# A recurrent layer with routed experts on one core: second relus of left-over expert jobs on ScalarE, a later lay-out of the extra slots, and four output buffers

## The chip, the cores and the metric

One core of a Trainium2 chip runs the whole program. The metric is the device time of one execution in microseconds, and the numbers compared are medians over several executions. All arithmetic is in 32-bit floats but for a few small tables in bf16. Engines are named as the profile names them: PE is TensorE (PEld its weight loads), DVE is VectorE, ACT is ScalarE, POOL is GpSimd, SP is SyncE; ACTq, SPq are the DMA queues that ACT and SP issue to.

## What is computed

The input is 8 sequences of 512 tokens with 128 features. Each layer half is preceded by a layer norm with a scale and a shift that depend on the sequence, and its output is multiplied by a gate and added to the input.

```python
for each of 512 time steps:                      # 8 sequences at once
    h_ssm = silu(h_ssm @ A.T + bx)               # 64 states
    r, z  = sigmoid(...), sigmoid(...)
    n     = tanh(i_n + r * h_n)
    h_rnn = (1 - z) * n + z * h_rnn              # 128 states
    out   = g0 * (h_ssm @ Cw.T + Cb + dx) + g1 * (h_rnn @ proj_w.T + proj_b)
x = x + ga * out
h = layernorm(x) * (1 + cb) + sb
expert_idx = argmax(softmax(h @ gate_w.T))       # one of 8 experts for each of 4096 tokens
y = relu(h @ w1[e] + b1[e]) @ w2[e] + b2[e]      # 128 -> 512 -> 128
x = x + gb * y * prob[e]
```

## The kernel before

**Steps and tiles.** The time steps are a chain, so the program is written as a loop over steps u (`steps`, U_END = 622 of them). Steps 0 to 511 each do one recurrent step; 16 of them make a tile of 128 tokens (16 steps by 8 sequences), tile c being steps 16c to 16c+15. Norms, routing and expert work of earlier tiles are placed by tables of step numbers into the steps of later tiles. From step 512 on there is no recurrence, only the rest of the expert work; I call these steps the tail. Every engine runs its own instruction list in the order in which the loop emits it, and the engines are held together by semaphores alone: a step number is a place in the lists, not a time.

**Experts.** Tiles 0 to 30 are dispatched in five groups (SIZE = 6, 7, 7, 6, 5). Each token's row is scattered by POOL into a block of its expert in a DRAM table (`rows`). A slot is one 128-row block of one expert. Slots 0 to 53 serve groups 0 to 3; in the last group slots 54 to 61 are fixed, one for each expert, and 62 to 65 are the extra slots, whose experts are found at run time. Tile 31 isn't scattered: each expert is applied to it whole and the results are gated and summed in `acc`.

**A slot's units.** On PE a slot is nine matmul units: X transposes the rows, A and C are the first layer in two halves, D and B the second layer; each of A, B, C, D has a first (hid_bank_a, hid_a) and a second part (hid_bank_b, hid_b). The table UNITS (`schedule`) says which units stand in which step. After X, ACT copies the bank to xT. After each A and C part a relu leaves PSUM: the first part always on ACT (L787), the second on DVE (L1176) unless the unit is in the set ON_ACT, which sends it to ACT (L783). After B, DVE adds the bias and evicts to y_sb (L1190), and SP stores it to `rows` (`store_y`, L623). Units are planned in `schedule` one by one while the recurrence runs; what is left of a group at step 512 (here the left-over jobs: slots 49 to 53 of group 3) is listed from step 512 on, three units a step, and the last group from step 526, mostly two a step.

**Lay-out.** Ten small DVE instructions per group (`lay_out`, L1055 to L1088: over, n_slots, end_slot, passed, expert_f, ended, first_f, block_f, place, expert) find the experts and blocks of the slots. `dispatch_at` gives their steps. `rows_at` is the step after them, from which SP loads (`load_expert`, L589 on): it reads the expert number, copies that expert's weights from w_all to wx (578 KB, L599), reads the block number and loads the rows (L604 or L607). SP's list is in order, so a store of y_sb listed behind such a load leaves after it. The rows of the fixed slots (`load_fixed`, L615) stand at step 513.

**Results.** A finished group is gathered by POOL, tile by tile, into yg (`gather`, four buffers; it first waits until all of the group's y_sb stores have landed). DVE makes fin_g (L1196) and o_sb (L1201) in steps FINAL_AT and OUT_AT; the tile is stored three steps later, in the tail by ACT (`store_out`, L854). o_sb has two buffers, so the o_sb of tile j waits for the store of tile j-2.

```python
def dispatch_at(k, n):
    at = (last_tile(k) + 2) * T
    return at + (2 + n if at < NT * T else 1 + n // 3)
```

Of the kernel before, what the change touches and what calls it, by code (L numbers as in the profile page):

```python
# [88 lines left out]
NBUF = 7  # L89
ND = 4  # L90
RING = 12
W_EXP = 2 * FC * P + FC + P

ENDED = (2, 2, 0, 0, 0, 0, 0, 0, 0, 1, 1, 0, 0, 0, 1, 0)
# [56 lines left out]
def dispatch_at(k, n):  # L151

    at = (last_tile(k) + 2) * T
    return at + (2 + n if at < NT * T else 1 + n // 3)


def scatter_at(j):
# [3 lines left out]
def rows_at(k):  # L161
    return dispatch_at(k, DISPATCH_STEPS - 1) + 1
# [19 lines left out]
def schedule():  # L182

    at, on_act, ready, act_ops, dve_used, relu_open = {}, set(), {}, {}, {}, set()

    def may(event, u, place):
        return event in ready and ready[event] <= (u, place)  # L190

    def ok(unit, u, place, first):
        kind, n, h = unit
        new = n == first
        if kind == "X":
            return new or may(("C", n - 1, 0), u, place)
        if kind == "A":
            return may(("X", n, 0), u, place) and (new or (may(("C", n - 1, h), u, place) and ("D", n - 1, h) in ready))
        if kind == "C":
            return may(("A", n, h), u, place) and ("A", n, 1) in ready and (new or ("B", n - 1, h) in ready)  # L200
        if kind == "D":
            return may(("A", n, h), u, place) and (new or may(("B", n - 1, 1), u, place))
        return may(("C", n, h), u, place) and ("D", n, 1) in ready

    def dve_room(u):
        return 270 if u // T < DVE_EARLY.get(u % T, 0) else DVE_ROOM[u % T]

    def home(unit, u, place):


        kind, n, h = unit
        if kind == "D" or unit[0::2] == ("B", 0):
            return "PE"
        if (kind == "B" or kind != "X" and h) and dve_used.get(u, 0) + DVE_COST[kind == "B"] <= dve_room(u):
            return "DVE"
        if kind != "B" and act_ops.get(u + (place > 0), 0) < ACT_ROOM[(u + (place > 0)) % T]:
            return "ACT"
        return None

    u = 0  # L220
    for k in range(NG - 1):
        first, end = SLOT0[k], SLOT0[k + 1]
        head = {"X": [], "A": [], "B": [], "C": [], "D": []}
        for unit in order_of_units(k):
            head[unit[0]].append(unit)
        u = max(rows_at(k) + 4, u)
        while any(head.values()) and u < NT * T:
            place = 0
            while place < ROOM - taken(u):
                for kind in PICK[place > 0]:  # L230
                    unit = head[kind][0] if head[kind] else None
                    where = home(unit, u, place) if unit and ok(unit, u, place, first) else None
                    if where:
                        break
                else:
                    break
                head[kind].pop(0)
                at.setdefault(u, []).append(unit)
                ready[unit] = (u, place + 1)
                if where == "ACT":  # L240
                    act_ops[u + (place > 0)] = act_ops.get(u + (place > 0), 0) + 1
                    ready[unit] = (u + (place > 0) + 1, 0)
                    if unit[2]:
                        on_act.add(unit)
                if where == "DVE":
                    dve_used[u] = dve_used.get(u, 0) + DVE_COST[kind == "B"]
                    ready[unit] = (u + 1, 1)
                if kind in "AC" and unit[2]:
                    relu_open.update(range(u, ready[unit][0] + ready[unit][1]))
                place += 1  # L250
            u += 1


    def room(u):
        return 3 if u < NT * T + T else 2

    u, used = NT * T, 0
    for k in range(NG):
        if rows_at(k) + 4 > u:
            u, used = rows_at(k) + 4, 0  # L260
        for i, what in enumerate(order_of_units(k)):
            if what in ready:
                continue
            if i == 1:
                u, used = u + 1, 0
            while used >= room(u):
                u, used = u + 1, 0
            at.setdefault(u, []).append(what)
            used += 1
    return at, on_act, relu_open  # L270


# [19 lines left out]
def final_steps():  # L292


    gather, final, u, f = {}, {}, 0, 0
    for k in range(NG):
        done = Y_STEP[SLOT0[k + 1] - 1]
        for i in range(SIZE[k]):
            u = max(u + 1, done + 4)
            if u < NT * T:  # L300
                u += min((14 - u) % T, (5 - u) % T if k >= 2 else T)
            if u >= NT * T:
                u = max(u, gather[FIRST[k] + i - 1] + (9 if k < NG - 1 else 3), NT * T + 13)
            gather[FIRST[k] + i] = u
            f = max(f + 1, u + (4 if u < NT * T else 12))
            final[FIRST[k] + i] = f
    return gather, final

# [9 lines left out]
def adaln_kernel(nc, x, silu_in, weights, ssm_weights, w1, b1, w2, b2, col_bias, bias_a, bias_b,  # L318
                 bias_const, const, out):
    ctx = ExitStack()  # L320
    with ctx:
        def sb(name, shape, dt=F32):
            return ctx.enter_context(nc.sbuf_tensor(name, shape, dt))
# [4 lines left out]
        def sem(name):  # L328
# [103 lines left out]
        y_sb = sb("y_sb", [P, NBUF, P])  # L432
        yg = sb("yg", [P, 4, P])
        fin_g = sb("fin_g", [P, P])
        o_sb = sb("o_sb", [P, 2, P])
        gate = sb("gate", [P, E])
        acc = sb("acc", [P, P])

# [55 lines left out]
        gate_ready, acc_step = sem("gate_ready"), sem("acc_step")  # L494
        w2_done, y_ready, fin_step, o_ready, stored = (
            sem("w2_done"), sem("y_ready"), sem("fin_step"), sem("o_ready"),
            [sem("stored0"), sem("stored1")])

        def ge(eng, s, n):

# [61 lines left out]
        def _(eng):  # L562
# [71 lines left out]
            def step(u, c, q, t):  # L634
# [11 lines left out]
                for j in range(NS):  # L646
                    if u == OUT_AT[j] + 3 and OUT_AT[j] < TAIL:
                        ge(eng, o_ready, j + 1)
                        eng.dma_start(out[:, j * P:(j + 1) * P], o_sb[:, j % 2, :]).then_inc(stored[j % 2], 16)

            steps(step)
            for q in range(2):
                eng.wait_ge(stored[q], 16 * NT // 2)


        @block.gpsimd
# [73 lines left out]
        def _(eng):  # L730
# [120 lines left out]
            def store_out(j):  # L851

                ge(eng, o_ready, j + 1)
                eng.dma_start(out[:, j * P:(j + 1) * P], o_sb[:, j % 2, :]).then_inc(stored[j % 2], 16)  # L854

            eng.wait_ge(seed_step, SEED_STEPS)
            eng.wait_ge(bank_filled, 3)
# [15 lines left out]
        def _(eng):  # L873
# [216 lines left out]
            def step(g, c, q, t):  # L1090
# [101 lines left out]
                for j in range(NS):  # L1192
# [4 lines left out]
                                                       in1=mod_gb, op0=ALU.mult, op1=ALU.mult).then_inc(fin_step, 1)  # L1197
                    if g == OUT_AT[j]:
                        ge(eng, fin_step, j + 1)
                        ge(eng, stored[j % 2], 16 * (j // 2))  # L1200
                        nc.vector.tensor_tensor(o_sb[:, j % 2, :], fin_g[:, :], x_sb[:, j * P:(j + 1) * P],  # L1201
                                                ALU.add).then_inc(o_ready, 1)

            steps(step)
# [2 lines left out]
            ge(eng, o_ready, j)  # L1207
            nc.vector.tensor_tensor(fin_g[:, :], acc[:, :], mod_gb, ALU.mult).then_inc(fin_step, 1)
            ge(eng, fin_step, j + 1)
            ge(eng, stored[j % 2], 16 * (j // 2))  # L1210
            nc.vector.tensor_tensor(o_sb[:, j % 2, :], fin_g[:, :], x_sb[:, j * P:(j + 1) * P],
                                    ALU.add).then_inc(o_ready, 1)


# [290 lines left out]
```

## Time and profile before

| | |
|---|---|
| median of 3 runs | 701.41 us (700.33 to 702.38) |
| profiled execution, its own time | 703.28 us |
| its span | 701.3 us |
| busy PE / PEld / DVE / ACT / POOL | 98% / 92% / 76% / 61% / 17% |
| PE's matmul instructions | 13868 |
| granted clock of PE, mean | 0.995 |
| chain that ended last, share of PE | 95% |

Times of rows are microseconds from the start of the span. "Busy" is time inside instructions; the part in brackets at a row's end is how long the engine had been idle before it, and what released it. PE rows merge neighbours of one kind, and a row x4 is one unit. The last recurrent step ends at 633.5; the tail is the rest.

### The profile page before, as it was taken

The numbers are of one execution on the slowest core, as the hardware profiler recorded it, in microseconds if no ns is written. First come the engines' busy times: TensorE is split into PE (matmuls) and PEld (weight loads), VectorE is DVE, ScalarE is ACT, GpSimd is POOL, SyncE is SP. The second block draws the span as 40 slices with busy tenths as digits, with TensorE's granted clock in tenths as the row PEclk, the third lists the DMA queues.
The fourth block names the chain that finished last, engine by engine and source line by source line (L and its number), as shares of the span: only waits on it lengthen the run. The fifth ranks groups of instructions, "written<-read, shape, count | busy, mean of one in ns | idle before, by whom it ended". The sixth has DMA issues, their size and how long they took to land.

```text
span 701.3 us, 35723 instructions
## 1 busy us (share of the span) xinstructions
PE 685.8 (98%) x13868; PEld 643.3 (92%) x13868; DVE 535.9 (76%) x3226; ACT 427.4 (61%) x2678; POOL 121.2 (17%) x209
## 2 busy tenths in 40 slices
PE   7999999999999999999999999999999999998896
PEld 5899999999999999999999999999999999997795
DVE  4777777777787777887888788878877878877455
ACT  4555555555766666567666665766667666664342
POOL 4011111111101111112121112121212122211202
PEclk9999999999999999999999999999999999999998
DMA  8915000604431100054221001633110353333411
GB/s 303 364 72 207 7 7 7 243 10 156 165 123 60 43 15 11 14 207 168 97 93 56 22 19 49 240 127 111 55 63 15 127 176 105 101 105 129 131 47 51
DMA packets 45659, 71.97 MB, mean 103 GB/s; under 512 B 6157, under 2 KB 28499, under 8 KB 45363
## 3 DMA queue, kind: packets, MB, share of 16 engines
q1 hardware_dynamic: 41490, 64.38, 26.1%
q0 software_dynamic: 1984, 4.07, 2.1%
q8 instruction: 110, 1.80, 1.1%
q10 hardware_dynamic: 2016, 1.25, 0.6%
q14 instruction: 59, 0.48, 0.2%
HBM read 14.31 MB, written 21.04 MB: 50 GB/s over the span
## 4 chain that ended last, share of the span: by engine, by line
PE 95%; DMA 1%; DVE 1%; SPq 1%; issue 1%; ACT 0%; POOLq 0%; DVEq 0%
PE rs_bank L1220 34%; PE nz_bank L1220 24%; PE hid_bank_b L1220 12%; PE work L1220 11%; PE y_bank L1220 8%; PE hid_bank_a L1220 7%; DMA out<-o_sb 1%; DMA yg<-rows,pos 0%; SPq L623 0%; DMA rows<-y_sb 0%; DVE fin_g L1196 0%; DVE hid_b L1176 0%; SPq L599 0%; SPq L598 0%; SPq L602 0%
## 5 line engine op out<-in xcount | busy, mean ns | idle before, releaser
L1220 PE MATMUL nz_bank<-h_ring,wg 128*64 128x16 f32 x4088 | 207.2, 211 | 0.0
L1220 PE MATMUL rs_bank<-s_ring,ws_sb 128*64 128x128 f32 x1024 | 195.1, 272 | 0.0
L795 ACT ACTIVATE r_fac<-rs_bank 128x8 f32<-128x8 f32 x512 | 91.6, 179 | 168.7 <-PE rs_bank L1220 161.6
L1220 PEld LDWEIGHTS nz_bank<-h_ring,wg 128*64 128x64 f32 x4088 | 160.7, 136 | 1.6
L1220 PE MATMUL rs_bank<-mw,wg 128*64 128x8 f32 x2044 | 146.7, 202 | 0.0
L1220 PE MATMUL rs_bank<-u,wg 128*64 128x8 f32 x2044 | 140.3, 206 | 0.0
L1220 PEld LDWEIGHTS rs_bank<-s_ring,ws_sb 128*64 128x64 f32 x1024 | 127.2, 136 | 9.1
L1101 DVE TENSOR_TENSOR_SCAN nz_bank<-r_fac,nz_bank 128x16 f32<-128x16 f32 x512 | 99.7, 195 | 46.2 <-ACT r_fac L795 30.4
L1105 DVE SCALAR_TENSOR_TENSOR mw<-v_fac,h_ring 128x8 f32<-128x8 f32 x512 | 85.6, 167 | 57.8
L1220 PEld LDWEIGHTS rs_bank<-mw,wg 128*64 128x64 f32 x2044 | 103.2, 135 | 18.9 <-DVE mw L1105 4.9
L801 ACT ACTIVATE v_fac<-nz_bank 128x8 f32<-128x8 f32 x512 | 91.1, 178 | 42.3
L1220 PEld LDWEIGHTS rs_bank<-u,wg 128*64 128x64 f32 x2044 | 101.8, 135 | 1.0
L1112 DVE SCALAR_TENSOR_TENSOR h_ring<-mw,u 128x8 f32<-128x8 f32 x512 | 85.4, 167 | 17.4
L803 ACT ACTIVATE n_fac<-nz_bank 128x8 f32<-128x8 f32 x512 | 91.0, 178 | 1.7
L1109 DVE SCALAR_TENSOR_TENSOR u<-v_fac,n_fac 128x8 f32<-128x8 f32 x512 | 85.6, 167 | 2.0
L798 ACT ACTIVATE s_ring<-rs_bank 64x8 f32<-64x8 f32 x512 | 80.9, 158 | 0.4 <-PE rs_bank L1220 0.4
L1220 PE MATMUL hid_bank_b<-w_sb,const_sb 128*64 128x128 f32 (+1 forms) x592 | 74.9, 322 | 0.0
L692 POOL DMA_INDIRECT rows<-h_ring,pos x31 | 31.7, 1022 | 243.9 <-DVE h_ring L1112 241.2
L676 POOL TENSOR_TENSOR ve<-mv,eps 128x1 f32<-128x1 f32 x64 | 16.9, 265 | 224.9 <-DVE mv L888 224.9
L787 ACT ACTIVATE hid_a<-hid_bank_a,wx 128x128 f32<-128x128 f32 x116 | 42.6, 367 | 11.0 <-PE hid_bank_a L1220 9.8
L1220 PE MATMUL hid_bank_b<-xT,wx 128*64 128x128 f32 x464 | 47.7, 280 | 1.0 <-DVE hid_b L1176 1.0
L1220 PE MATMUL hid_bank_a<-xT,wx 128*64 128x128 f32 x464 | 48.1, 281 | 0.2
(181 smaller groups left out, 1129.1 us busy)
## 6 DMA issues: line engine op xcount, KB each, us to landing
wx<-w_all SPq DMA_DIRECT2D x58, 578.0 KB, 3.5
rows<-zeros SPq DMA_DIRECT2D x3, 4096.0 KB, 14.5
rows<-y_sb SPq DMA_DIRECT2D x66, 64.0 KB, 1.8
w_all<-in_w SPq DMA_DIRECT2D x2, 2048.0 KB, 15.4
xs_sb<-rows SPq DMA_DIRECT2D x54, 64.0 KB, 3.0
x_sb<-in_x SPq DMA_DIRECT2D x1, 1920.0 KB, 8.8
out<-o_sb SPq DMA_DIRECT2D x19, 64.0 KB, 2.5
out<-o_sb ACTq DMA_DIRECT2D x13, 64.0 KB, 1.5
```

What stands on the lines that cost most here:

```text
L676: nc.gpsimd.tensor_tensor(ve[:, :], mv[:, 1:2], eps[:, :], ALU.add).then_inc(ve_done, 1)
L692: nc.gpsimd.indirect_dma_start(rows[k % 3].ap(), index(pos, j), h2_ring[:, j % RING, :], None).then_inc(scattered[k % 3], 16)
L787: nc.scalar.activation(hid_a[:, h, :], hid_bank[0][:, 0:P], ACT.Relu, bias=bias1(i, 2 * h)).then_inc(relu_a_ready, 1)
L795: nc.scalar.activation(r_fac[:, k, :, 1], r_cols(q, t), ACT.Tanh, scale=0.5).then_inc(rn_ready, 1)
L798: nc.scalar.activation(s_ring[0:SSM, pq, pt, 0:B], s_cols(g - 1), ACT.Silu).then_inc(hs_ready, 1)
L801: nc.scalar.activation(v_fac[:, k, :], z_cols(q, t), ACT.Tanh, scale=-0.5).then_inc(sig_ready, 1)
L803: nc.scalar.activation(n_fac[:, k, :], n_pairs(q, t)[:, :, 1], ACT.Tanh).then_inc(tanh_ready, 1)
L1101: nc.vector.tensor_tensor_scan(pairs, r_fac[:, k, :, :].rearrange("p b k -> p (b k)"), pairs, 0.0, ALU.mult, ALU.add).then_inc(pre_n_ready, 1)
L1105: nc.vector.scalar_tensor_tensor(out=mw[:, k, :], in0=v_fac[:, k, :], scalar=1.0, in1=h_ring[:, pq, pt, :], op0=ALU.subtract, op1=ALU.mult ...
L1109: nc.vector.scalar_tensor_tensor(out=u[:, k, :], in0=v_fac[:, k, :], scalar=1.0, in1=n_fac[:, k, :], op0=ALU.add, op1=ALU.mult).then_inc(u ...
L1112: nc.vector.scalar_tensor_tensor(out=h_ring[:, q, t, :], in0=mw[:, k, :], scalar=-0.5, in1=u[:, k, :], op0=ALU.mult, op1=ALU.add).then_inc ...
L1220: last = nc.tensor.matmul(out[c:c + COLS], weights[:, c:c + COLS], moving, start=start, stop=stop, skip_group_check=skip_group_check)
```

## The change

It has four parts. In the functions spoken of here, line numbers of the changed file are one to three higher.

- The second relus of units A and C of the left-over jobs, slots 49 to 53 (ten instructions), go into ON_ACT and so from DVE to ACT.
- The lay-out of the last group moves from steps 513 to 516 to steps 525 to 529, two instructions a step. Its `rows_at` thereby goes from 517 to 530. The planner's condition `k < NG - 1` keeps the fixed slots' units where they were: PE's list does not change.
- Tile 19's fin_g and o_sb move from step 514 to 530 (its gather stays at 510). No other tile's steps change.
- o_sb has four buffers (NO = 4) with a semaphore each.

```diff
@@ dispatch_at
-    return at + (2 + n if at < NT * T else 1 + n // 3)
+    return at + (2 + n if at < NT * T else 13 + n // 2)
@@ schedule
-        if rows_at(k) + 4 > u:
+        if k < NG - 1 and rows_at(k) + 4 > u:
             u, used = rows_at(k) + 4, 0
...
             at.setdefault(u, []).append(what)
             used += 1
+            if k < NG - 1 and what[0] in "AC" and what[2]:
+                on_act.add(what)
@@ final_steps
-            f = max(f + 1, u + (4 if u < NT * T else 12))
+            f = max(f + 1, u + (4 if u < NT * T else 12), NT * T + 18 if u + 4 >= NT * T else 0)
@@ buffers, stores and waits (the same in SP, ACT and DVE code)
+NO = 4
-        o_sb = sb("o_sb", [P, 2, P])
+        o_sb = sb("o_sb", [P, NO, P])
-            [sem("stored0"), sem("stored1")])
+            [sem(f"stored{b}") for b in range(NO)])
-                eng.dma_start(out[:, j * P:(j + 1) * P], o_sb[:, j % 2, :]).then_inc(stored[j % 2], 16)
+                eng.dma_start(out[:, j * P:(j + 1) * P], o_sb[:, j % NO, :]).then_inc(stored[j % NO], 16)
-                        ge(eng, stored[j % 2], 16 * (j // 2))
-                        nc.vector.tensor_tensor(o_sb[:, j % 2, :], fin_g[:, :], x_sb[:, j * P:(j + 1) * P],
+                        ge(eng, stored[j % NO], 16 * (j // NO))
+                        nc.vector.tensor_tensor(o_sb[:, j % NO, :], fin_g[:, :], x_sb[:, j * P:(j + 1) * P],
```

DVE's list before, from slot 49's second relu in step 512 to step 514 (over to ended is the lay-out, y_sb the eviction of slot 48, fin_g and o_sb tile 19's output):

```order
L1176 TENSOR_SCALAR hid_b<-hid_bank_b,wx 128x128
L1061 TENSOR_TENSOR over<-next_row,block_row 128x8x5
L1065 TENSOR_REDUCE n_slots<-over 128x8
L1067 SCALAR_TENSOR_TENSOR end_slot<-ones_e,n_slots 128x8
L1190 TENSOR_TENSOR y_sb<-y_bank,wx 128x128
L1176 TENSOR_SCALAR hid_b<-hid_bank_b,wx 128x128
L1119 TENSOR_SCALAR g_sb<-g_raw 128x2
L1071 TENSOR_TENSOR passed<-end_slot,count 128x32
L1074 TENSOR_REDUCE expert_f<-passed 128x4
L1076 TENSOR_TENSOR ended<-passed,end_slot 128x32
L1196 SCALAR_TENSOR_TENSOR fin_g<-yg,prob,mod 128x128
L1201 TENSOR_TENSOR o_sb<-fin_g,x_sb 128x128
```

With the change all of these but y_sb and g_sb are gone from there.

DVE's list with the change, from tile 31's gate in step 525 to step 528 (y_sb evicts slot 52, then slot 53; hid_b is slot 54's relu, acc tile 31's sum):

```order
L1148 TENSOR_SCALAR gate<-onehot,prob 128x8
L1064 TENSOR_TENSOR over<-next_row,block_row 128x8x5
L1068 TENSOR_REDUCE n_slots<-over 128x8
L1193 TENSOR_TENSOR y_sb<-y_bank,wx 128x128
L1070 SCALAR_TENSOR_TENSOR end_slot<-ones_e,n_slots 128x8
L1074 TENSOR_TENSOR passed<-end_slot,count 128x32
L1077 TENSOR_REDUCE expert_f<-passed 128x4
L1079 TENSOR_TENSOR ended<-passed,end_slot 128x32
L1193 TENSOR_TENSOR y_sb<-y_bank,wx 128x128
L1155 TENSOR_SCALAR acc<-w_all,gate 128x128
L1081 TENSOR_REDUCE first_f<-ended 128x4
L1083 SCALAR_TENSOR_TENSOR block_f<-expert_f,first_f 128x4
```

and on through steps 529 and 530, place, expert and tile 19's output being the added rows:

```order
L1179 TENSOR_SCALAR hid_b<-hid_bank_b,w_all 128x128
L1157 SCALAR_TENSOR_TENSOR acc<-w_all,gate,acc 128x128
L1087 TENSOR_TENSOR place<-block_f,count 128x4
L1090 TENSOR_SCALAR expert<-expert_f 128x4
L1157 SCALAR_TENSOR_TENSOR acc<-w_all,gate,acc 128x128
L1179 TENSOR_SCALAR hid_b<-hid_bank_b,w_all 128x128
L1199 SCALAR_TENSOR_TENSOR fin_g<-yg,prob,mod 128x128
L1204 TENSOR_TENSOR o_sb<-fin_g,x_sb 128x128
```

The ten lay-out instructions and two output instructions now stand between the evictions and relus of steps 525 to 530.

SP's list before, from the fixed slots' rows on (rows0<-y_sb are the stores of slots 48 and 49, then 50, then 51 to 53; each expert, wx, place, xs_last is one of the four extra slots' loads):

```order
L615 DMA xs_last<-rows1 128x128 x8
L623 DMA rows0<-y_sb 128x128 x2
L598 TENSOR_LOAD expert
...
L604 DMA xs_last<-rows1 128x128
L623 DMA rows0<-y_sb 128x128
L598 TENSOR_LOAD expert
...
L604 DMA xs_last<-rows1 128x128
L623 DMA rows0<-y_sb 128x128 x3
L623 DMA rows1<-y_sb 128x128 x12
```

and with the change:

```order
L618 DMA xs_last<-rows1 128x128 x8
L626 DMA rows0<-y_sb 128x128 x6
L601 TENSOR_LOAD expert
...
L607 DMA xs_last<-rows1 128x128
L626 DMA rows1<-y_sb 128x128 x12
```

All stores of group 3 (rows0) now stand before the four loads, and all stores of the last group (rows1) still behind them.

## Rows read from the trace of the kernel before

**Rows 1.** Busy time by stretch: stretch, length, engines' busy us, PEclk, DMA share, GB/s.
```profile
659.20:662.00 2.80, 0.16 (x4) 0.10 (x4) 1.06 (x4) 0.00 (x0) 2.00 (x3) 1.00 0.19 47
662.00:667.00 5.00, 5.00 (x61) 4.89 (x63) 2.00 (x7) 1.78 (x6) 1.89 (x2) 0.66 0.28 69
667.00:677.00 10.00, 9.93 (x173) 9.17 (x171) 6.13 (x19) 4.35 (x14) 0.95 (x1) 1.00 0.20 54
```

**Rows 2.** PE in order of time, 639 to 649: start us, us, line, [idle before <-releaser].
```profile
639.14 0.44 PE L1220 MATMUL hid_bank_b<-xT,wx 128*64 128x128 f32 x4 [1.00 <-DVE hid_b L1176]
...
643.88 0.44 PE L1220 MATMUL work<-w_sb,h2T 128*64 128x128 f32 x4 [0.36 <-ACT h2T L825]
...
648.08 0.44 PE L1220 MATMUL y_bank<-wx,hid_a 128*64 128x128 f32 x4 [0.80 <-DVE y_sb L1190]
```

**Rows 3.** DVE in order of time, 635 to 648, the same columns.
```profile
635.18 0.22 DVE L1061 TENSOR_TENSOR over<-next_row,block_row 128x40 f32<-128x40 f32 x1
635.50 0.18 DVE L1065 TENSOR_REDUCE n_slots<-over 128x8 f32<-128x32 f32 x1
...
637.25 0.35 DVE L1196 SCALAR_TENSOR_TENSOR fin_g<-yg,prob,mod 128x128 f32<-128x128 f32 x1
...
638.74 0.34 DVE L1176 TENSOR_SCALAR hid_b<-hid_bank_b,wx 128x128 f32<-128x128 f32 x1
...
645.03 0.35 DVE L1176 TENSOR_SCALAR hid_b<-hid_bank_b,wx 128x128 f32<-128x128 f32 x1
...
647.74 0.28 DVE L1190 TENSOR_TENSOR y_sb<-y_bank,wx 128x128 f32<-128x128 f32 x1
```

**Rows 4.** ACT in order of time, around 632.
```profile
631.86 0.36 ACT L783 ACTIVATE hid_b<-hid_bank_b,wx 128x128 f32<-128x128 f32 x1
632.11 0.27 ACT L780 COPY xT<-hid_bank_a 128x128 f32<-128x128 f32 x1
```

**Rows 5.** DVE in order of time, 649 to 658.
```profile
649.22 0.29 DVE L1190 TENSOR_TENSOR y_sb<-y_bank,wx 128x128 f32<-128x128 f32 x1 [0.94 <-PE y_bank L1220]
...
650.73 0.81 DVE L1154 SCALAR_TENSOR_TENSOR acc<-w_all,gate,acc 128x128 f32<-128x128 f32 x2
651.46 0.35 DVE L1176 TENSOR_SCALAR hid_b<-hid_bank_b,w_all 128x128 f32<-128x128 f32 x1
...
652.43 0.34 DVE L1176 TENSOR_SCALAR hid_b<-hid_bank_b,w_all 128x128 f32<-128x128 f32 x1
...
657.42 0.35 DVE L1176 TENSOR_SCALAR hid_b<-hid_bank_b,w_all 128x128 f32<-128x128 f32 x1 [0.18 <-PE hid_bank_b L1220]
```

**Rows 6.** SP's DMA issues in order of time, 642 to 685.
```profile
642.92 0.50 SPq L599 DMA_DIRECT2D wx<-w_all  x1
...
645.75 0.50 SPq L599 DMA_DIRECT2D wx<-w_all  x1
...
653.46 31.34 SPq L623 DMA_DIRECT2D rows<-y_sb  x15
```

**Rows 7.** Chain of waits, 655 to 661: start us, us, what.
```profile
655.65 1.76 DMA rows<-y_sb
...
658.31 2.57 DMA yg<-rows,pos
```

**Rows 8.** PE in order of time, 658 to 662.
```profile
658.88 0.39 PE L1220 MATMUL hid_bank_a<-h2T,w_all 128*64 128x128 f32 x4
661.90 0.44 PE L1220 MATMUL hid_bank_b<-h2T,w_all 128*64 128x128 f32 x4 [2.64 <-DVE hid_b L1176]
```

**Rows 9.** DVE in order of time: eviction of slot 61's result.
```profile
673.53 0.29 DVE L1190 TENSOR_TENSOR y_sb<-y_bank,w_all 128x128 f32<-128x128 f32 x1
```

**Rows 10.** DVE in order of time, 696 to 700.
```profile
696.18 0.29 DVE L1201 TENSOR_TENSOR o_sb<-fin_g,x_sb 128x128 f32<-128x128 f32 x1 [1.00 <-DMA out<-o_sb]
...
698.14 0.29 DVE L1201 TENSOR_TENSOR o_sb<-fin_g,x_sb 128x128 f32<-128x128 f32 x1 [0.37 <-DMA out<-o_sb]
...
698.98 0.29 DVE L1211 TENSOR_TENSOR o_sb<-fin_g,x_sb 128x128 f32<-128x128 f32 x1 [0.15 <-DMA out<-o_sb]
```

More of the change, by code:

```diff
@@ L648, in step @@
                         ge(eng, o_ready, j + 1)
-                        eng.dma_start(out[:, j * P:(j + 1) * P], o_sb[:, j % 2, :]).then_inc(stored[j % 2], 16)
+                        eng.dma_start(out[:, j * P:(j + 1) * P], o_sb[:, j % NO, :]).then_inc(stored[j % NO], 16)
             steps(step)
-            for q in range(2):
-                eng.wait_ge(stored[q], 16 * NT // 2)
+            for q in range(NO):
+                eng.wait_ge(stored[q], 16 * NT // NO)
         @block.gpsimd
@@ L853, in store_out @@
                 ge(eng, o_ready, j + 1)
-                eng.dma_start(out[:, j * P:(j + 1) * P], o_sb[:, j % 2, :]).then_inc(stored[j % 2], 16)
+                eng.dma_start(out[:, j * P:(j + 1) * P], o_sb[:, j % NO, :]).then_inc(stored[j % NO], 16)
             eng.wait_ge(seed_step, SEED_STEPS)
@@ L1209, in _ @@
             ge(eng, fin_step, j + 1)
-            ge(eng, stored[j % 2], 16 * (j // 2))
-            nc.vector.tensor_tensor(o_sb[:, j % 2, :], fin_g[:, :], x_sb[:, j * P:(j + 1) * P],
+            ge(eng, stored[j % NO], 16 * (j // NO))
+            nc.vector.tensor_tensor(o_sb[:, j % NO, :], fin_g[:, :], x_sb[:, j * P:(j + 1) * P],
                                     ALU.add).then_inc(o_ready, 1)
```

## The prediction

> **What bounds the kernel now.** I read the shares first, then the chain of waits, then stretches, then each engine in order of time where the stretches show idle time. PE is 98% busy and carries 95% of the chain that ended last, and the change takes no matmul away. So it can gain only where PE waits, where its clock is low, or after its last instruction. The recurrence I cost at nothing: the lists of all engines are the same up to step 511, and the only waits of o_sb for a store that the trace shows are three behind its end [rows 10].
>
> In the tail I find five places:
>
> - PE is idle for 1.00 us before a second matmul of a layer (slot 50's), released by a second relu on DVE [rows 2]. That relu starts at 638.74 only, behind fin_g at 637.25, its o_sb, tile 31's mix and three lay-out instructions [rows 3].
> - PE is idle for 0.80 us before 648.08, waiting for the eviction of slot 52 at 647.74 [rows 2, 3].
> - PE is idle for 2.64 us before 661.90 [rows 8]. The relu named there stood behind tile 20's fin_g, that behind tile 20's gather, and the gather behind the store of slot 53, whose landing ends at 657.41 (655.65 + 1.76) [rows 7]. Slot 53 had been evicted on DVE by 649.5 (649.22 + 0.29) [rows 5]; its store stood in SP's list behind loads for extra slots, which take 2.83 us each (645.75 - 642.92), and left in the series that begins at 653.46 [rows 6].
> - Right behind this pause the granted clock is 0.66 over five microseconds, and 1.00 again after it [rows 1].
> - After PE's last matmul DVE waits three times for a store to free one of two output buffers: 1.00, 0.37 and 0.15 us [rows 10].
>
> **1. Relus to ACT, lay-out and tile 19's output away from DVE (steps 512 to 526): 1.3 us gained.** The 1.00 us goes: the relu no longer stands behind anything on DVE, and on ACT only the first relu of the same unit stands ahead of it. Is ACT then late? Ten relus more on ACT: a relu and the copy behind it start 0.25 us apart [rows 4], PE's units follow each other by 0.22 us, so the copy xT, which stands behind two relus in place of one, starts 0.03 us later in each of four slots. The relu itself costs 0.36 us there against 0.34 to 0.35 on DVE [rows 3, 4]. I cost both at nothing.
>
> From tile 31's logits on PE at 643.88 to slot 53's first second-layer unit at 648.08 lie 4.20 us [rows 2], and they are a chain on DVE: maximum, difference, one-hot, sn, reciprocals, gate, eviction. In this list two relus of 0.35 us go, the one at 645.03 [rows 3] and the one of the unit after it. Two lay-out instructions come in ahead of the eviction: the second starts 0.32 us after the first, since it reads it [rows 3], and holds DVE for about 0.1 us more. That is 0.70 - 0.42 = 0.3 us. In all 1.3 us. The bounds: 0.3 us if the 1.00 us turns up at the next wait on that chain, 2.0 us if the 0.80 us at its end goes nearly whole.
>
> **2. What the lay-out and tile 19's output cost in their new place (steps 526 to 530): 0.55 us lost.** Cover is thin here. From the relu at 651.46 to the one at 652.43 DVE is full with two steps of tile 31's sum, which need 0.81 us for two because each reads the other [rows 5]. The fixed slots have two units a step, so a late relu reaches PE at once. Six instructions come in: first_f, block_f, place, expert, fin_g and o_sb. The first two fall where DVE is idle ahead of slot 54's relu, and place and expert mostly into the gaps between dependent sums. fin_g and o_sb (0.35 and 0.29 us, [rows 3, 10]) stand fully behind slot 54's last relu and ahead of slot 55's: 0.64 us, less 0.1 for overlap. Bounds: 0.2 us if PE has slack that I don't see, 1.3 us if all six (four of 0.17, and these two) lie bare.
>
> **3. The stores of group 3 leave before the loads: 2.8 us gained.** Slot 53's eviction ends at 649.5, less 1.3, at 648.2. SP has nothing ahead of its store, which lands 1.8 us later (1.76, [rows 7]), at 650.0. The gather started 0.9 us after the landing (657.41 to 658.31) and took 2.57 us [rows 7]; now it would end at 653.5. DVE comes to tile 20's fin_g at 657.7 in the old trace (the relu before it begins at 657.42 and lets the next instruction start 0.27 us later) [rows 5], so at 656.9 now. The gather is 3.4 us early. PE's unit at 661.90 would follow the one at 658.88 by 0.22 us instead of 3.02 [rows 8]: 2.8 us. What is late next is nothing new: the gathers of tiles 21 to 23 follow without a wait for these stores, since tile 19's output, which tile 23's gather asks for, is done by about 652.
>
> What is made late by it: the lay-out ends at about 650 in place of 639.4, so the four loads run from 650.8 to 662.1 (4 x 2.83), and the stores of slots 54 to 57 wait behind them. The first to need one is the eviction of slot 61 into the same y buffer, at 673.53 [rows 9], some 5 us earlier now, at 668.5. Slot 54's store has landed at 663.9. It is covered by 4.6 us; the rows of slot 62 are needed later still.
>
> **4. The clock: 1.7 us gained.** A mean of 0.66 over 5.00 us is 3.4 us at the lower of the two levels, 1.2 in place of 2.4 GHz, and as PE was busy all through [rows 1], half of these 3.4 us was lost. After the pause of 1.00 us [rows 2] no stretch showed a lower clock. With no pause longer than about 1 us left I expect none. Nothing if it falls all the same.
>
> **5. Four buffers: 1.3 us gained.** The three waits are 1.52 us [rows 10]. Tile 28's output then only follows its fin_g, and tile 31's last one waits for tile 27's store, long landed. I keep back 0.2 us, because expert 7's product leaves PE no earlier, and because more stores are in flight when the last is issued. Bounds: 0.4 us if tile 30's gather, which cannot start before tile 26's output, takes its place as the wait, 1.5 us if nothing does.
>
> By the Trainium skill (DMA: Bandwidth & Descriptors, "Queues, rings and completion order") a transfer's semaphore lands only after every earlier write of the same DMA engine, across its queues. By that, tile 20's gather could not report before the first 578 KB expert load issued beside it; that is the third rival below, and no row here shows it alone.
>
> **Sum.** 1.3 - 0.55 + 2.8 + 1.7 + 1.3 = 6.5 us. The profiled execution would go from 703.28 to 696.8 us. It stands 1.9 us above the median of the runs, which I take as the same offset for both, so the median goes from 701.4 to **694.9 us**.
>
> **Rivals.**
>
> - *ACT becomes the bound of the left-over jobs* (0.10). For it: C's second relu stands directly ahead of xT, and xT is what each slot's first unit waits for. Against it: the spacing of 0.25 us [rows 4]. If relus do not overlap and follow each other by 0.36 us, each slot takes 0.2 us longer, 1.0 us over five: 695.9 us. The Trainium skill (ScalarE: Activation LUTs, "Rules for kernel authors") says to use VectorE, not ScalarE, for relu, for its speed per element above all in bf16. Here the tiles are 32-bit and in PSUM, and the two rows differ by 0.01 to 0.02 us: the trace does not bear the rule out for this shape, but it is why this rival has a tenth.
> - *The clock falls in another place* (0.08), after a wait that I have not seen: the 1.7 us stay lost, 696.6 us.
> - *Tile 20's gather is late all the same* (0.06), held up by the expert load that now starts at the same time as it. It decides if the gather takes over 2.57 + 3.4 = 6.0 us. Terms 3 and 4 are then lost: 699.4 us.
> - *Slower: the stores of the last group come too late* (0.03). In SP's list twelve stores stand behind four loads that now start 11 us later. If a load took 5.6 us in place of 2.83, slot 54's store would land 11.1 us later, at 675.0, and the 4.6 us of cover and the gain of 6.5 us would be used up; PE would then stand at slot 61's eviction. At 6 us a load the stores are 12.7 us late, 8.1 more than the cover, and the time is 694.9 + 8.1 = 703.0 us. Against it: the same loads took 2.83 us in the same tail, and nothing makes them twice as dear.
> - *No change* (0.03): the waits in the tail are there but another chain of equal length stands behind each (tile 31's own layer norm and routing, then PE's order). Within 0.3% of 701.4.
>
> The forecast itself has 0.70. Its own bounds, added, are 3.9 us (0.3 - 1.3 + 2.8 + 1.7 + 0.4) and 7.8 us (2.0 - 0.2 + 2.8 + 1.7 + 1.5), so 697.5 to 693.6 us; the runs before scatter by 1 us to either side. I take 693.0 to 698.2, which holds the first two rivals too. A measurement of this kernel tells 0.3%, about 2 us, from no change. All cases but the last two are faster by about that or more: 0.94 faster, 0.03 the same, 0.03 slower.
>
> **What the profile would show.** Right: no idle over 0.5 us before a hid_bank_b unit between 634 and 644; slot 53's D unit near 646.8; PE without a pause over 1 us up to its end; clock 1.00 throughout the tail; a single series of six stores before the four loads on SP; no wait of o_sb for a store; PE's last unit near 690, the last o_sb near 692.5. Wrong: PE idle before hid_bank_a units behind xT would mean the first rival; a row fin_g released by a gather near 657 the third; y_sb released by a store near 668 the fourth. Term 2 is wrong if PE shows no pauses behind DVE's relus around 651.

## The result and the profile after

The changed kernel takes **696.82 us** (median of 6 runs, 696.40 to 698.74), the kernel before beside it 702.69 us (6 runs, 700.33 to 704.16). The ratio is 0.9912, its 95% interval 0.9892 to 0.9932: 5.9 us, or 0.9%, faster. Forecast were 694.9 us in a range of 693.0 to 698.2, and a gain of 6.5 us. Later runs of the kernel before put its median at 702.7 to 703.3 us, so the three runs of before that I had (median 701.41 us) were among its shorter ones.

The profiled execution took 697.02 us, its span is 695.2 us (703.28 and 701.3 before). Below are three lines of the page of the changed kernel: PE's busy time, its granted clock in 40 slices, and the shares of the chain that ended last.

```profile
PE 684.6 (98%) x13868; PEld 641.9 (92%) x13868; DVE 533.8 (77%) x3216; ACT 429.5 (62%) x2688; POOL 121.0 (17%) x209
...
PEclk9999999999999999999999999999999999999999
...
PE 97%; DVE 1%; issue 0%; ACT 0%; DVEq 0%
```

PE's matmul count is the same as before, and it is busy for 1.2 us less (685.8 before). I read nothing from that difference: the lighter kernel below, also at full clock in the tail, has 683.0. In the chain the two transfers, the store into `rows` and the gather, are gone: it is PE nearly throughout.

PE in order of time: slot 50's second unit; tile 31's logits; slot 53's first D unit; the one unit left in the tail that waits for a late relu (0.25 us); and tile 31's two units around the old pause.

```profile
638.32 0.43 PE L1223 MATMUL hid_bank_b<-xT,wx 128*64 128x128 f32 x4
...
643.13 0.44 PE L1223 MATMUL work<-w_sb,h2T 128*64 128x128 f32 x4 [0.35 <-ACT h2T L828]
...
646.91 0.44 PE L1223 MATMUL y_bank<-wx,hid_a 128*64 128x128 f32 x4 [0.27 <-DVE y_sb L1193]
...
652.44 0.44 PE L1223 MATMUL hid_bank_b<-xT,w_all 128*64 128x128 f32 x4 [0.25 <-DVE hid_b L1179]
...
658.48 0.39 PE L1223 MATMUL hid_bank_a<-h2T,w_all 128*64 128x128 f32 x4
658.70 0.39 PE L1223 MATMUL hid_bank_b<-h2T,w_all 128*64 128x128 f32 x4
```

The first row answers to the one with 1.00 us idle in [rows 2], and has no idle time; the third to 648.08 with 0.80 us, now 0.27; the last two to [rows 8], now 0.22 us apart, where they were 3.02 apart. The clock where it had been 0.66 [rows 1] is now 1.00 (stretch, length, busy us of PE, PEld, DVE, ACT, POOL, PEclk, DMA share, GB/s):

```profile
661.00:666.00 5.00, 5.00 (x90) 4.68 (x88) 3.15 (x10) 2.27 (x8) 0.95 (x1) 1.00 0.70 233
666.00:676.00 10.00, 9.93 (x174) 9.23 (x170) 6.27 (x20) 4.49 (x14) 0.00 (x0) 1.00 0.14 40
```

SP's DMA issues, and the start of tile 20's gather on POOL:

```profile
641.52 7.18 SPq L626 DMA_DIRECT2D rows<-y_sb  x6
651.01 0.50 SPq L602 DMA_DIRECT2D wx<-w_all  x1
...
654.28 0.50 SPq L602 DMA_DIRECT2D wx<-w_all  x1
...
662.10 17.91 SPq L626 DMA_DIRECT2D rows<-y_sb  x12
```

```profile
650.96 1.00 POOL L704 DMA_INDIRECT yg<-rows,pos  x1 [10.57 <-issue]
```

The six stores of group 3 now leave in one series as soon as each slot is evicted, the four loads follow, and the twelve stores of the last group wait behind them until 662.10. The forecast had 662.1 for that and 650.9 for the gather; tile 20's fin_g starts at 657.29 without idle time. This is the new place of the last two lay-out instructions (place, expert) and of tile 19's output on DVE, between relus (hid_b), and at the end tile 20's fin_g:

```profile
649.30 0.35 DVE L1179 TENSOR_SCALAR hid_b<-hid_bank_b,w_all 128x128 f32<-128x128 f32 x1 [0.39 <-PE hid_bank_b L1223]
...
649.83 0.15 DVE L1087 TENSOR_TENSOR place<-block_f,count 128x4 int32<-128x4 f32 x1
650.09 0.17 DVE L1090 TENSOR_SCALAR expert<-expert_f 128x4 int32<-128x4 f32 x1
...
650.47 0.34 DVE L1179 TENSOR_SCALAR hid_b<-hid_bank_b,w_all 128x128 f32<-128x128 f32 x1
650.73 0.34 DVE L1199 SCALAR_TENSOR_TENSOR fin_g<-yg,prob,mod 128x128 f32<-128x128 f32 x1
651.11 0.29 DVE L1204 TENSOR_TENSOR o_sb<-fin_g,x_sb 128x128 f32<-128x128 f32 x1
651.32 0.80 DVE L1157 SCALAR_TENSOR_TENSOR acc<-w_all,gate,acc 128x128 f32<-128x128 f32 x2
652.04 0.34 DVE L1179 TENSOR_SCALAR hid_b<-hid_bank_b,w_all 128x128 f32<-128x128 f32 x1
...
657.29 0.34 DVE L1199 SCALAR_TENSOR_TENSOR fin_g<-yg,prob,mod 128x128 f32<-128x128 f32 x1
```

And the end, which answers to [rows 10]: the outputs (o_sb) of tiles 28, 29, 30 and 31 without a wait for a store.

```profile
690.42 0.29 DVE L1204 TENSOR_TENSOR o_sb<-fin_g,x_sb 128x128 f32<-128x128 f32 x1
...
691.32 0.29 DVE L1204 TENSOR_TENSOR o_sb<-fin_g,x_sb 128x128 f32<-128x128 f32 x1
...
692.09 0.29 DVE L1204 TENSOR_TENSOR o_sb<-fin_g,x_sb 128x128 f32<-128x128 f32 x1
692.49 0.29 DVE L1211 TENSOR_TENSOR fin_g<-acc,mod 128x128 f32<-128x128 f32 x1
692.82 0.29 DVE L1214 TENSOR_TENSOR o_sb<-fin_g,x_sb 128x128 f32<-128x128 f32 x1
```

**One measure for all kernels.** The profiled executions do not enter the tail at the same time: PE's first tail matmul (work<-bias_bf) starts between 632.86 and 634.73 in the twelve profiles of this study, though the recurrence is the same code. So I cut the tail at six PE rows and one DVE row and compare the pieces; in (a), (b) and (c) equal code gives equal pieces to 0.04 us, and in (e) too at equal clock, but for 0.17 us that some kernels have and others not, at one place near slot 60, which I leave open. Pieces that contain a wait for a transfer are less exact: with code that is the same up to there, (d) is 3.02 in before and 3.33 in four_buffers, and with two output buffers (f) lies between 3.24 and 4.00. (a) from the first tail matmul to tile 31's logits, (b) to slot 53's first D unit, (c) to the hid_bank_a unit of [rows 8], (d) to the unit after it, (e) to PE's last unit, (f) to the last o_sb. All are start to start, in us.

| kernel | a | b | c | d | e | f | sum |
|---|---|---|---|---|---|---|---|
| before | 9.96 | 4.20 | 10.80 | 3.02 | 33.08 | 4.00 | 65.06 |
| changed | 8.95 | 3.78 | 11.57 | 0.22 | 31.48 | 2.64 | 58.64 |
| changed, second profile | 8.95 | 3.78 | 11.57 | 0.21 | 31.50 | 2.63 | 58.64 |
| relus_only | 9.13 | 3.36 | 10.80 | 4.49 | 32.86 | 3.79 | 64.43 |
| loads_later | 10.00 | 4.19 | 10.80 | 0.21 | 31.66 | 3.65 | 60.51 |
| four_buffers | 9.97 | 4.19 | 10.80 | 3.33 | 33.08 | 2.63 | 64.00 |
| filled_pause | 10.00 | 4.19 | 10.80 | 3.34 | 31.53 | 3.24 | 63.10 |
| fin19_early | 8.95 | 3.77 | 10.98 | 0.22 | 31.49 | 2.63 | 58.04 |
| relus_back | 8.75 | 4.60 | 11.57 | 0.22 | 31.49 | 2.63 | 59.26 |
| lighter | 8.95 | 3.36 | 10.80 | 0.22 | 31.65 | 2.63 | 57.61 |
| outputs_earlier | 8.94 | 3.36 | 10.80 | 0.22 | 31.38 | 2.67 | 57.37 |

The lighter kernel's second profile is within 0.01 us of its first. The tail is 6.42 us shorter with the change; 0.26 us of the span are lost in when it begins, 0.06 us after the last o_sb.

**The clock in the timed executions.** For every execution the mean granted clock is on record. The slow stretch of [rows 1], 1.7 us lost of 701.3, would by itself lower that mean to 0.998. Of the 45 later executions of the kernel before, 32 have 0.997 or less, with a median of 703.3 us, but 13 have 0.999 (700.76 to 702.39 us, median 701.7). So in 13 of 45 the clock cannot have been low over the whole stretch, with the same code. The three kept traces of kernels with two or more microseconds of pause and no filling (before, relus_only, four_buffers) all show the stretch; none was kept of an execution without it, so what decides it stays open.

### The profile page after: what moved, and what is told of

Its sections match the earlier page's. It is cut to its first block, busy times and chain, and to the rows that moved or that the text cites. A ratio compares the mean times of both kernels' runs of the same rounds, so it can differ in the third digit from the quotient of the medians.

```text
span 695.2 us, 35722 instructions
## 1 busy us (share of the span) xinstructions
PE 684.6 (98%) x13868; PEld 641.9 (92%) x13868; DVE 533.8 (77%) x3216; ACT 429.5 (62%) x2688; POOL 121.0 (17%) x209
## 4 chain that ended last, share of the span: by engine, by line
PE 97%; DVE 1%; issue 0%; ACT 0%; DVEq 0%
PE rs_bank L1223 34%; PE nz_bank L1223 24%; PE hid_bank_b L1223 12%; PE work L1223 11%; PE y_bank L1223 9%; PE hid_bank_a L1223 7%; DVE fin_g L1199 0%; DVE acc L1157 0%; DVE o_sb L1204 0%; DVE hid_b L1179 0%; ACT xT L783 0%; ACT hid_a L790 0%; DVE prob L1023 0%; DVE y_sb L1193 0%; DVE fin_g L1211 0%
```

## The experiments

### Only the relus

Slots 49 to 53's second relus on ACT, nothing else:

```diff
             used += 1
+            if k < NG - 1 and what[0] in "AC" and what[2]:
+                on_act.add(what)
```

> The kernel before with only the ten second relus of slots 49 to 53 on ACT. My theory: the three gains in the middle of the tail hang together, because tile 20's gather is released by slot 53's store, and that by SP's list, not by PE. So slot 53's second-layer unit comes 1.5 us or more earlier than 648.08 (two relus gone from the DVE chain and no lay-out added to it), but the pause before 661.90 grows from 2.64 us to 3.5 to 4.3 us, the clock still falls behind it, and the time is that of before within 1 us. Rival: the pause moves forward with PE, and the kernel gains about 1.5 us by itself.

Measured: 700.90 us against 702.68, ratio 0.9982 (0.9969 to 0.9995). PE's row at slot 53's first D unit, the unit ahead of the pause, and the one behind it:

```profile
646.64 0.44 PE L1222 MATMUL y_bank<-wx,hid_a 128*64 128x128 f32 x4
...
657.44 0.39 PE L1222 MATMUL hid_bank_a<-h2T,w_all 128*64 128x128 f32 x4
661.93 0.70 PE L1222 MATMUL hid_bank_b<-h2T,w_all 128*64 128x128 f32 x4 [4.10 <-DVE hid_b L1178]
```

Slot 53 comes 1.67 us sooner after the first tail matmul (a + b is 12.49 in place of 14.16), and (d), the pause, takes 1.47 us of it back: 4.49 in place of 3.02. Its end hardly moves (661.93, before 661.90), as it must if SP's list sets it. The clock falls, and at once: the row behind the pause is already a slow one (0.70 us for a unit that takes 0.39 to 0.44 at full clock). At the end of the pause 0.2 us are left of the whole first term; the tail as a whole is 0.6 us shorter, the rest being 0.22 us in (e) and 0.21 us in (f), which varies anyway. The timed ratio says 0.4 to 2.2 us, and the median lies 1.8 us below before's, past the 1 us that I had allowed. By its time alone the rival (1.5 us gained) would do as well; it is the trace that speaks against it, since the pause did not move forward with PE.

### Only the loads

SP's four loads listed at step 530, the lay-out where it was:

```diff
-    return dispatch_at(k, DISPATCH_STEPS - 1) + 1
+    return dispatch_at(k, DISPATCH_STEPS - 1) + 1 if k < NG - 1 else NT * T + 18
...
-        if rows_at(k) + 4 > u:
+        if k < NG - 1 and rows_at(k) + 4 > u:
```

> The kernel before with only SP's four loads of the extra slots listed at step 530, behind all stores of group 3; lay-out, relus, tile 19's output and the two output buffers stay. My theory: the order of SP's list is the whole cause of the pause and of the low clock behind it, so the pause before the fixed slots' unit is gone, the clock stays at 1.00 and the time falls by 2.8 + 1.6 = 4.4 us. PE still waits 1.0 us for a relu near 639 and 0.8 us for slot 52's eviction, and the stretch from slot 53's D unit to tile 31's second first-layer unit keeps its 10.8 us. Rival: DVE's load in steps 513 to 516 is what makes slot 53 late; then the pause stays at over 1.5 us.

Measured: 698.04 us, ratio 0.9929 (0.9911 to 0.9947), which is 3.7 to 6.3 us. PE at the same places, and slot 50's unit:

```profile
638.32 0.44 PE L1220 MATMUL hid_bank_b<-xT,wx 128*64 128x128 f32 x4 [1.00 <-DVE hid_b L1176]
...
658.08 0.39 PE L1220 MATMUL hid_bank_a<-h2T,w_all 128*64 128x128 f32 x4
658.29 0.39 PE L1220 MATMUL hid_bank_b<-h2T,w_all 128*64 128x128 f32 x4
```

The idle 1.00 us on DVE's account is there, and the pause of 2.64 us is gone. The tail is 4.55 us shorter: 2.81 from the pause, 1.42 from the clock, 0.35 from the end (within what (f) varies with two buffers). So DVE's load is not what made tile 20's gather late; the order of SP's list is enough, and it is most of what the change gains.

### Only the buffers

```diff
+NO = 4
-        o_sb = sb("o_sb", [P, 2, P])
+        o_sb = sb("o_sb", [P, NO, P])
```

and j % NO for j % 2 in the stores and waits.

> The kernel before with only four output buffers in place of two. My theory: from the start of PE's last matmul group to the start of the last o_sb go 2.6 us in place of 4.0, the time falls by 1.4 us, nothing else moves. Rival: tile 30's gather or the ACT queue holds the output instead, and the gain stays under 0.5 us.

Measured: 700.88 us, ratio 0.9964 (0.9951 to 0.9977). The outputs of tiles 28 to 31 on DVE:

```profile
696.33 0.29 DVE L1202 TENSOR_TENSOR o_sb<-fin_g,x_sb 128x128 f32<-128x128 f32 x1
...
697.23 0.29 DVE L1202 TENSOR_TENSOR o_sb<-fin_g,x_sb 128x128 f32<-128x128 f32 x1
...
698.01 0.29 DVE L1202 TENSOR_TENSOR o_sb<-fin_g,x_sb 128x128 f32<-128x128 f32 x1
...
698.73 0.29 DVE L1212 TENSOR_TENSOR o_sb<-fin_g,x_sb 128x128 f32<-128x128 f32 x1
```

None has an idle part, where three had one in [rows 10]: piece f is 2.63 in place of 4.00 us, 1.37 less, against 1.3 forecast. The 4.00 us are the longest end of the four profiles with two buffers; the others have 3.79 (relus_only), 3.65 (loads_later) and 3.24 us (filled_pause), so the buffers are worth 0.6 to 1.4 us from one execution to the next. The timed ratio asks for 1.6 to 3.4 us, more than the pieces give (1.06, since the pause came out 0.31 us longer). I have no cause for the rest, and where the tail begins varies by as much. Two of its ten executions have a granted clock of 1.000, and they are its shortest (698.61 and 699.14 us).

### The pause filled

To see if the low clock follows from the pause, PE was kept busy in it: 11 dummy units into a bank that the next unit but one overwrites. They add work, and the pause itself stays.

```diff
+                    if dense and e == 0 and kind == "C" and second:
+                        ge(eng, h_ready, NT * T)
+                        for _ in range(11):
+                            mm(nz_bank[0][:, 0:P], ident, w_sb[:, W_MOD:W_MOD + P], start=True, stop=True)
                     ge(eng, (relu_a_ready, relu_b_ready)[second], 2 * i + h)
```

> The kernel before, with eleven dummy 128-column matmul units (2.4 us) on PE in the pause before 661.90, at the place where it waits for the relu behind tile 20's output; the pause itself stays. My theory: the low clock is the consequence of the pause, so with PE busy in it the clock stays at 1.00, the stretch from the unit after the pause to PE's last one takes 31.65 us in place of 33.08, and the time falls by 1.4 us. Rival: the clock falls there for another reason and the stretch keeps 33.0 us, with no gain.

PE in order of time, and the stretch behind it:

```profile
658.19 0.39 PE L1220 MATMUL hid_bank_a<-h2T,w_all 128*64 128x128 f32 x4
658.41 2.57 PE L1220 MATMUL nz_bank<-w_sb,const_sb 128*64 128x128 f32 x44
661.53 0.44 PE L1220 MATMUL hid_bank_b<-h2T,w_all 128*64 128x128 f32 x4 [0.55 <-DVE hid_b L1176]
```

```profile
664.00:669.00 5.00, 5.00 (x90) 4.68 (x87) 3.25 (x11) 2.15 (x7) 0.95 (x1) 1.00 0.24 67
```

The same ten units, from the first slow one of before to the first at full clock again, in before and here:

```profile
663.14 0.59 PE L1220 MATMUL nz_bank<-w_all,hid_a 128*64 128x128 f32 x4
...
666.77 0.42 PE L1220 MATMUL y_bank<-w_all,hid_a 128*64 128x128 f32 x4
```

```profile
662.76 0.42 PE L1220 MATMUL nz_bank<-w_all,hid_a 128*64 128x128 f32 x4
...
664.85 0.42 PE L1220 MATMUL y_bank<-w_all,hid_a 128*64 128x128 f32 x4
```

The 44 matmul records are the dummies. Only 0.55 us of idle time is left, the clock stays at 1.00, the ten units take 2.09 us from start to start in place of 3.63, and piece e is 31.53 us in place of 33.08. In these traces the low clock was the consequence of the pause, at a price of 1.4 (loads_later) to 1.6 us (here and in the changed kernel). The time is 702.24 against 703.27 us, ratio 0.9990 (0.9973 to 1.0007), which is anything from 1.9 us gained to 0.5 us lost. So the timed runs neither show the 1.4 us nor rule them out; of the 15 executions of before beside it only nine have a clock of 0.997 or less, and only those can have the whole stretch to win back.

### Tile 19's output out of the crowded place

The changed kernel with the 18 in `final_steps` set to 6, so that tile 19's fin_g and o_sb stand in step 518:

> The changed kernel with tile 19's output at step 518 in place of 530; the lay-out stays in steps 525 to 529. My theory (my second term): most of the 0.77 us that the stretch from slot 53's D unit to tile 31's second first-layer unit has lost is fin_g and o_sb of tile 19, so 11.57 us become 10.95 to 11.05. The stretch from PE's first tail matmul to the logits keeps 8.95. Rival: the lay-out's six late instructions cost most of it, and 11.3 us or more are left.

Slot 53's D unit and tile 31's unit ahead of the old pause, on PE:

```profile
645.72 0.44 PE L1223 MATMUL y_bank<-wx,hid_a 128*64 128x128 f32 x4 [0.26 <-DVE y_sb L1193]
...
656.70 0.39 PE L1223 MATMUL hid_bank_a<-h2T,w_all 128*64 128x128 f32 x4
```

Piece c is 10.98 in place of 11.57. So tile 19's output cost 0.59 us there and the lay-out the other 0.18. The kernel was executed once, 695.25 us, so only the pieces are read.

### The relus back on DVE

The changed kernel without the two added lines of `schedule`:

> The changed kernel with the ten second relus of slots 49 to 53 on DVE again. My theory: the pause of 1.00 us before slot 50's second unit had two causes, either of which would have removed it alone, since lay-out and tile 19's output have left DVE there too: no pause over 0.3 us comes back and the logits stand 9.0 to 9.2 us behind the first tail matmul (8.95 with the relus on ACT, 9.96 before). From the logits to slot 53's D unit the two relus on DVE cost again 0.8 us: 4.6 us in place of 3.78. Rival: the relus alone made the pause, and the first stretch goes back to over 9.6 us.

Logits and slot 53's first D unit on PE:

```profile
642.89 0.44 PE L1221 MATMUL work<-w_sb,h2T 128*64 128x128 f32 x4 [0.36 <-ACT h2T L826]
...
647.49 0.44 PE L1221 MATMUL y_bank<-wx,hid_a 128*64 128x128 f32 x4 [1.21 <-DVE y_sb L1191]
```

The pause of 1.00 us does not come back: a is 8.75 us, below the 9.0 to 9.2 that I expected and even 0.20 less than with the relus on ACT. The DVE chain from the logits on is 0.82 us longer. So moving ten relus is worth 0.62 us here (59.26 against 58.64), not 1.4: they help only in the chain behind the logits and cost 0.2 ahead of it. The pause needed two things at once, the relu on DVE and the lay-out and tile 19's output ahead of it there, and it ends when either is gone: relus_only took away the one, this kernel the other. It was executed once, 697.62 us.

### A version without the loss

If the relus are on ACT, DVE has idle time early in the tail. So: the changed kernel with the lay-out in its old steps, the loads at step 530 as in loads_later, and tile 19's output at step 518.

```diff
-    return at + (2 + n if at < NT * T else 13 + n // 2)
+    return at + (2 + n if at < NT * T else 1 + n // 3)
...
-    return dispatch_at(k, DISPATCH_STEPS - 1) + 1
+    return dispatch_at(k, DISPATCH_STEPS - 1) + 1 if k < NG - 1 else NT * T + 18
...
-            f = max(f + 1, u + (4 if u < NT * T else 12), NT * T + 18 if u + 4 >= NT * T else 0)
+            f = max(f + 1, u + (4 if u < NT * T else 12), NT * T + 6 if u + 4 >= NT * T else 0)
```

> The changed kernel with the lay-out back in steps 513 to 516, SP's loads still listed at step 530, and tile 19's output at step 518 in place of 530. My theory: with the relus gone DVE has idle time from 634 to 641, which takes the ten lay-out instructions and tile 19's output for nothing, while in steps 525 to 530 they cost PE 0.8 us, and over and n_slots ahead of slot 52's eviction 0.4 us. So from PE's first tail matmul to slot 53's D unit 12.3 us in place of 12.7, from there to tile 31's second first-layer unit 10.8 in place of 11.6, and the time about 1.2 us below the changed kernel's, 695.6. Rival: the lay-out in front delays tile 31's layer norm, which then holds PE at its transpose, and the gain is under 0.5 us.

Measured: 694.71 us (4 runs, 694.66 to 695.00) against 702.68, ratio 0.9885 (0.9867 to 0.9903). Logits, slot 53's D unit and tile 31's unit on PE:

```profile
641.81 0.44 PE L1223 MATMUL work<-w_sb,h2T 128*64 128x128 f32 x4 [0.35 <-ACT h2T L828]
...
645.17 0.44 PE L1223 MATMUL y_bank<-wx,hid_a 128*64 128x128 f32 x4
...
655.97 0.39 PE L1223 MATMUL hid_bank_a<-h2T,w_all 128*64 128x128 f32 x4
```

b is 3.36 and c 10.80: both losses are gone, and a keeps its 8.95, so the layer norm does not suffer. I ran it once more beside the changed kernel.

> The changed kernel once more, on the same chip as the lighter one, so that the two can be compared directly. My theory: 1.0 to 1.2 us slower than the lighter kernel, all of it between the logits and tile 31's second first-layer unit (3.78 + 11.57 us against 3.36 + 10.80). Rival: the two agree within their scatter and the lighter one's lower median was the other session's.

> The lighter kernel once more, beside the changed one. My theory: 1.0 to 1.2 us faster than the changed kernel. Rival: no difference that the timed runs show.

Measured: 696.59 us for the changed kernel (ratio 0.9912, 0.9891 to 0.9934), 695.72 us for the lighter one (0.9903, 0.9879 to 0.9927). The medians differ by 0.9 us in the direction of the pieces (1.0 us), but the runs overlap (696.40 to 697.53, 694.53 to 697.56). The pieces repeat: 3.78 and 11.57 against 3.36 and 10.80. It beats both kernels in the trace; against the changed one the runs alone don't settle it.

### Outputs made earlier

The lighter kernel with the outputs of tiles 26 to 30 at fixed steps 603, 607, 609, 611, 612:

> The lighter kernel with the outputs of tiles 26 to 30 made at steps 603, 607, 609, 611 and 612 in place of 606 to 618. My theory: DVE idles for 0.64 us before every second relu of the dense experts, which is the length of one fin_g and one o_sb, and the gathers of tiles 26 to 29 have landed there; so only two or three outputs are left behind PE's last matmul, from there to the last o_sb go 1.9 us in place of 2.6, PE loses nothing or gains 0.2, and the time falls by 0.7 to 1.0 us to 693.8. Rival: the outputs stand in front of relus that PE waits for, or wait for a gather, and what is won at the end is lost before it.

Measured: 695.49 us against 703.27, ratio 0.9893 (0.9874 to 0.9913), no better than the lighter kernel's 0.9885, and 1.7 us above the 693.8 that I expected. Tile 29's o_sb and tile 30's fin_g on DVE:

```profile
687.82 0.29 DVE L1206 TENSOR_TENSOR o_sb<-fin_g,x_sb 128x128 f32<-128x128 f32 x1
688.95 0.35 DVE L1201 SCALAR_TENSOR_TENSOR fin_g<-yg,prob,mod 128x128 f32<-128x128 f32 x1 [0.84 <-DMA yg<-rows,pos]
```

PE's piece e is 0.27 us shorter. The end, for which I expected 1.9 us, keeps 2.67: when DVE comes to tile 30's fin_g its gather has not landed, and a wait of 0.84 us takes the place of the work that was moved. The rival's second half was right: the gather is the next bound of the end.

## Why the prediction was right

**The bound.** That the recurrence is untouched and all is decided by PE's waits, its clock and the work after its last unit held: the tail's pieces give 6.42 us, and 6.42 less the 0.26 and 0.06 us at its two ends are the 6.1 us between the spans.

**First term, 1.3 us.** Measured 1.43: 1.01 up to the logits and 0.42 behind them. Both halves were close, but the reason for the first was credited wrongly. The prediction let the 1.00 us go since the relu moved to ACT. In relus_back it goes as well with the relu on DVE. And relus on ACT were costed at nothing ahead of the logits; they cost 0.20 us over the three copies to xT that stand there, about 0.07 each where I had 0.03. In the chain behind the logits they are worth 0.82 us where I had 0.70, and the two lay-out instructions cost the 0.42 us that I had (3.36 against 3.78).

**Second term, a loss of 0.55 us.** Measured 0.77. The step that was off is "place and expert mostly into the gaps between dependent sums": fin_g and o_sb cost 0.59, as worked out, but the lay-out 0.18 more. In the rows above, the two relus around place and expert start 1.17 us apart (649.30, 650.47), where the same two were 1.00 apart before (650.46, 651.46): that is the lay-out's share, 0.18 but for rounding. From 650.47 to the next relu at 652.04 it is 1.57 us in place of 0.97, tile 19's share.

**Third term, 2.8 us.** Measured 2.80. loads_later shows it by itself. The gather started 0.1 us from the forecast time. That the size fits to the hundredth is luck: the same pause was 0.3 us longer in four_buffers and in filled_pause. One remark of this part is off without harm: the four loads start 8.1 us later than before (651.01 against 642.92), not 11 as the fourth rival says; 11 us is by how much the lay-out ends later.

**Fourth term, 1.7 us.** Measured 1.60 in the changed kernel, 1.42 to 1.55 in the kernels that part it from the rest. Half of the slow 3.4 us, 1.7, was a little too much: the same ten units give 3.63 - 2.09 = 1.54 us. At full clock one of these steps is 0.31 us (664.08 to 664.39 in filled_pause) in place of 0.22, while the low clock spaces them all by 0.43, which accounts for about 0.1 of the difference. And the term was put as if the clock fell in every execution; in 13 of 45 of the kernel before it did not, or not for so long, and there less than this term can be gained.

**Fifth term, 1.3 us.** Measured 1.36, and 1.37 alone, against a profile with the longest end of four; 0.6 to 1.4 against all of them. So the good fit of this term is partly the luck of the profiled execution.

**The sum.** 6.42 against 6.5 in the tail (the five terms add up to 6.55), with a term too small by 0.1 and a loss too small by 0.2 that offset each other in part; the timed ratio gives 4.8 to 7.6. The time came out 1.9 us above the forecast one; 1.3 of it are the start, since the median of 701.4 us that I subtracted from was that of three runs and is 702.7 with six, and 0.6 the gain. The step that did not hold is the offset of 1.9 us between profiled execution and median, "which I take as the same offset for both": the changed kernel's profiled execution, 697.02 us, was forecast to 0.2 us (696.8), but it stands only 0.2 us above its median.

**The terms don't add freely.** Alone, the first term leaves 0.2 us behind the pause (0.6 by the end of the tail), because the pause grows by nearly all of it; together with the third it is worth its full size.

**The rivals.** ACT as the bound of the left-over jobs: 0.2 us in place of 1.0, so a trace of it is there. The Trainium skill's rule for relu (ScalarE: Activation LUTs, "Rules for kernel authors") would have kept them on VectorE: for slots 49 to 51 the trace agrees by 0.2 us, for the relus in the chain behind the logits it doesn't, by 0.82, since what counts there is whose list is free. The clock did not fall elsewhere. Tile 20's gather was not late: it was issued at 650.96, 0.05 us from the first 578 KB load at 651.01, and DVE came to it 6.3 us later without a wait, so the Trainium skill's rule on completion order (DMA: Bandwidth & Descriptors, "Queues, rings and completion order") cost nothing here, and no row shows by how much it held. The stores of slots 54 to 57 left at 662.10 as worked out, and no eviction waited for one.

## What to carry to other kernels

Where a long wait ends in a transfer, look at what stands ahead of its issue in the issuing queue's list before looking at the engines: here four loads that nobody needed for over 20 us held one store, and with them listed later 4.4 of the 6.4 us are gained (2.8 the pause, 1.6 the clock behind it). Two late parts on one chain do not pay one by one, so judge a change of one of them by the piece of the trace, not by the end; and where a piece contains a wait for a transfer, take it from more than one execution. And work that is moved out of a full place should go where the receiving engine idles: the same twelve DVE instructions cost 1.2 us in one place and nothing twelve steps earlier.

## What the runs showed of the hardware

The idle time of PE of 2.64 us before 661.90 was followed by slow units from 663.14 on, at 1.2 GHz (granted clock 0.50); that of 2.94 us in four_buffers was too; after that of 4.10 us in relus_only the first unit was slow already (661.93, 0.70 us). Idle times of 1.00, 0.80 and, in relus_back, 1.21 us were followed by full clock, and so was the pause of filled_pause with PE busy for all but 0.55 us of it. The timed executions say that the low clock does not follow the shorter pause each time: 13 of 45 of the kernel before have a mean clock of 0.999, while all ten of relus_only have 0.997 or less. The tail of the changed kernel and that of the lighter one, each profiled twice, repeat to 0.02 us in every piece. Waits for transfers vary more, 0.3 us in the pause and 0.8 us at the end with two buffers, over kernels with the same code there. The start of the tail varies by 1.9 us over the twelve profiles, at a granted clock of 1.00 up to it. What makes it vary stays open.
